# Cross attention with 128 key columns and 128 value rows where there are 77 keys

## What is computed

```python
xn1 = _ln(x, g1, be1)
sa = _mha(xn1, xn1, Wq_s, bq_s, Wk_s, bk_s, Wv_s, bv_s, causal=True)
x = x + (sa @ W1 + b1)
xn2 = _ln(x, g2, be2)
ca = _mha(xn2, encoder_out, Wq_c, bq_c, Wk_c, bk_c, Wv_c, bv_c, causal=False)
x = x + (ca @ W2 + b2)
xn3 = _ln(x, g3, be3)
ff = jax.nn.relu(xn3 @ Wf1 + bf1) @ Wf2 + bf2
return x + ff
```

## Time and profile before

| | |
|---|---|
| median of 3 runs | 603.57 us (601.41 to 603.72) |
| the profiled execution | 601.15 us, its span 599.1 us |
| mean granted clock | 0.909 |
| TensorE busy | 509.2 us, 85% of the span |
| DVE, ACT, POOL busy | 336.7, 324.5, 186.7 us |
| scores of both attentions (line 1057) | 150.0 us in 448 matmuls |
| products of both attentions (line 1086) | 108.5 us in 896 instructions |

### The profile page before, as it was taken

How to read it: one execution, slowest core, us unless ns; L and a number is a source line. 1 busy time by engine, 2 the same in 40 slices (tenths; PEclk the granted TensorE clock), 3 DMA queues, 4 the chain that set the end, 5 groups by cost and what they waited for, 6 DMA issues and landing times.

```text
span 599.1 us, 8849 instructions
## 1 busy us (share of the span) xinstructions
PE 509.2 (85%) x3296; PEld 286.1 (48%) x3296; DVE 336.7 (56%) x645; ACT 324.5 (54%) x622; POOL 186.7 (31%) x288
## 2 busy tenths in 40 slices
PE   1598875999999999999988767769999677999887
PEld 1385642343434343434333235433334356988877
DVE  3165985887878787878732035554441456263340
ACT  3685311767766767676765641346664753354460
POOL 2497950122222222222231531232324273030200
PEclk9999995999999999999998998865555978999999
DMA  8145955033352435241205045764523310101001
GB/s 280 56 137 172 219 138 91 1 64 63 65 100 55 72 63 103 59 68 34 56 4 160 18 144 105 148 146 94 110 54 75 71 42 0 36 2 36 19 19 35
DMA packets 31082, 48.11 MB, mean 80 GB/s; under 512 B 8832, under 2 KB 25728, under 8 KB 28928
## 3 DMA queue, kind: packets, MB, share of 16 engines
q1 hardware_dynamic: 30904, 47.52, 34.4%
q10 hardware_dynamic: 136, 0.03, 0.0%
HBM read 30.66 MB, written 12.03 MB: 71 GB/s over the span
## 4 chain that ended last, share of the span: by engine, by line
PE 65%; DMA 9%; DVE 9%; ACT 8%; issue 3%; POOL 2%; SPq 1%; ACTq 0%; DVEq 0%
PE ps L1086 14%; PE ps L1057 13%; PE ps L965 11%; PE ps L1020 11%; PE ps L1173 8%; DMA stacks<-shift_t 4%; DVE max_a L1252 4%; PE ps L949 3%; ACT arena_p L823 3%; DMA sums<-out_t 2%; PE ps L1042 2%; PE ps L1024 2%; ACT out_t L834 2%; ACT xn L859 1%; DMA recips<-recip_rows 1%
## 5 line engine op out<-in xcount | busy, mean ns | idle before, releaser
L823 ACT ACTIVATE arena_p<-ps 128x512 f32<-128x512 f32 (+4 forms) x416 | 197.0, 538 | 125.2 <-PE ps L1057 122.3
L1252 DVE TENSOR_REDUCE max_a<-ps 128x1 f32<-128x512 f32 (+4 forms) x280 | 163.2, 621 | 73.7 <-PE ps L1020 58.5
L1057 PE MATMUL ps<-stacks 99*128 99x512 bf16 (+2 forms) x448 | 150.0, 370 | 19.8 <-DMA stacks<-shift_t 12.5
L1020 PE MATMUL ps<-stacks 96*128 96x77 bf16 (+4 forms) x640 | 142.1, 300 | 11.0 <-DVE max_a L1252 7.8
L1086 PE MATMUL ps<-arena_p,v_group 128*32 128x512 f32 (+4 forms) x896 | 108.5, 565 | 1.6 <-POOL arena_p L694 1.2
L1020 PEld LDWEIGHTS ps<-stacks 96*128 96x128 bf16 x640 | 58.5, 112 | 95.9 <-DVE max_a L1252 44.9
L694 POOL TENSOR_SCALAR_AFFINE_SELECT arena_p<-arena_p 128x512 f32<-128x512 f32 x64 | 39.9, 635 | 176.8 <-ACT arena_p L823 176.8
L1057 PEld LDWEIGHTS ps<-stacks 99*128 99x128 bf16 (+1 forms) x448 | 46.1, 108 | 82.3 <-ACT arena_p L823 45.6
L1252 DVE TENSOR_REDUCE max_b<-ps 128x1 f32<-128x384 f32 (+3 forms) x88 | 52.4, 634 | 6.6 <-PE ps L1024 6.6
L1232 DVE TENSOR_TENSOR xs<-ps,xs 128x512 f32<-128x512 f32 x24 | 16.4, 690 | 69.1 <-PE ps L965 45.5
L899 ACT ACTIVATE hid_r<-ps,col 128x512 fp32r<-128x512 f32 x32 | 22.0, 688 | 54.2 <-PE ps L1173 51.8
(11 more groups left out here) (70 smaller groups left out, 516.9 us busy)
## 6 DMA issues: line engine op xcount, KB each, us to landing
arena_h<-out_t SPq DMA_DIRECT2D x16, 256.0 KB, 5.4
recips<-recip_rows SPq DMA_DIRECT2D x8, 512.0 KB
q_parts<-parts SPq DMA_DIRECT2D x8, 384.0 KB, 2.7
k_parts<-parts SPq DMA_DIRECT2D x8, 384.0 KB, 2.9
qc_parts<-parts SPq DMA_DIRECT2D x8, 384.0 KB, 3.2
stacks<-qc_parts SPq DMA_DIRECT2D x8, 384.0 KB, 5.4
stacks<-q_parts SPq DMA_DIRECT2D x7, 384.0 KB, 5.0
stacks<-k_parts SPq DMA_DIRECT2D x7, 384.0 KB, 7.7
```

Of the source, the lines that this page charges most:

```text
L823: nc.scalar.activation(probs[0:a.kp, a.probs_slot(g, ui), h, k * BANK:k * BANK + width], ps[0:a.kp, unit % S_BANKS, 0:width], ACT.Exp, sca ...
L1020: ins = nc.tensor.matmul(m_bank(use)[:, o:o + w], q_stack[0:ROWS, g % a.nb, h, t * P:(t + 1) * P], k_rows(ROWS, g, h, s0, s0 + w), start=T ...
L1057: ins = nc.tensor.matmul(ps[0:keys, unit % S_BANKS, lo - k * BANK:hi - k * BANK], k_rows(ROWS_S, g, h, i * P, i * P + keys), q_stack[:, g ...
L1252: nc.vector.tensor_reduce(dst, m_bank(use)[:, 0:nh * w].rearrange("p (h w) -> p h w", h=nh), AX.X, ALU.max).then_inc(s.max_read, 1)
```

## The change

Cross attention's score matmuls take 128 columns of keys for their weights, in place of 77. The keys of all groups and heads lie one behind another (`k_ctx_row`, 77 columns a head), so the columns from the 78th on are those of the next head, or, for the last, of what self attention left there. The scores then fill all 128 partitions of the bank; ACT still reads 77 of them. The products take 128 rows of V and of probs, in place of 77. For this V is filled with zeros on partitions 64 to 127 before the ones and the values are written on the first 77; and a part of `probs` that nothing has written before is cleared once, ahead of self attention. The product waits for three steps of V in place of one.

```diff
--- before.py
+++ after.py
@@ -300,8 +300,8 @@
             arena_p = attention_only.enter_context(nc.sbuf_tensor("arena_p", [P, P_SLOTS * GH * T], F32))
         q_stack = stacks[:, 0:5, :, :]
         k_self = stacks[:, 3:6, :, :]
-        k_ctx = stacks[:, 5, :, :].rearrange("p h t -> p (h t)")[:, 0:NG * GH * S_CTX]\
-            .rearrange("p (g h t) -> p g h t", g=NG, h=GH)
+        k_ctx_row = stacks[:, 5, :, :].rearrange("p h t -> p (h t)")
+        k_ctx = k_ctx_row[:, 0:NG * GH * S_CTX].rearrange("p (g h t) -> p g h t", g=NG, h=GH)
         probs = arena_p[:, :].rearrange("p (s h t) -> p s h t", s=P_SLOTS, h=GH)
 
         wf2r = sb("wf2r", [P, 2, FF // P, C], F32R)
@@ -665,6 +665,11 @@
                         src = v_self[:, g, :, :].rearrange("p i (h d) -> p i h d", d=D)
                         dst = v_group[:, g % 2, :, :, 0::2]
                     else:
+
+                        pool.wait_ge(split_p, U_QC + 6)
+                        pool.memset(v_group[64:P, 0, :, :, :], 0.0).then_inc(s.v_set, 1)
+                        pool.wait_ge(s.v_set, 1)
+                        pool.memset(v_group[0:S_CTX, 0, :, :, 1::2], 1.0).then_inc(s.v_set, 1)
                         src = v_ctx[:, :, :].rearrange("p g (h d) -> p g h d", d=D)
                         dst = v_group[0:S_CTX, 0, :, :, 0::2]
                     pool.tensor_copy(dst, src).then_inc(s.v_set, 1)
@@ -739,6 +744,10 @@
             made(pool.memset(k_self[ROWS:ROWS_S, :, :, :], 1.0))
             pool.wait_ge(consts, 9)
             third_parts(*range(12, U_QC))
+            pool.wait_ge(acc_full, 2 * a_at["v", NCH - 1] + 2)
+            pool.wait_ge(split_p, U_QC)
+            made(pool.memset(probs[64:P, 2, :, SELF.steps[2][1]:T], 0.0))
+            pool.wait_ge(consts, 10)
             attention(SELF, S1)
             add_bias(NCH)
             add_bias(NCH + 1)
@@ -1053,9 +1062,10 @@
                     for i, q0, w, off in a.steps[ui][0]:
                         lo, hi = max(off, k * BANK), min(off + w, (k + 1) * BANK)
                         if lo < hi:
-                            keys = min(P, a.keys - i * P)
-                            ins = nc.tensor.matmul(ps[0:keys, unit % S_BANKS, lo - k * BANK:hi - k * BANK],
-                                                   k_rows(ROWS_S, g, h, i * P, i * P + keys),
+                            at = (g * GH + h) * S_CTX
+                            ins = nc.tensor.matmul(ps[:, unit % S_BANKS, lo - k * BANK:hi - k * BANK],
+                                                   k_rows(ROWS_S, g, h, i * P, (i + 1) * P) if a.causal
+                                                   else k_ctx_row[0:ROWS_S, at:at + P],
                                                    q_stack[:, g % a.nb, h, q0 + lo - off:q0 + hi - off],
                                                    start=True, stop=True)
                     ins.then_inc(s.scores, 1)
@@ -1073,7 +1083,7 @@
                     else:
                         pe.wait_ge(s.exps, len(a.units) * g + GH * (n + 1))
                     if ui == 0:
-                        pe.wait_ge(s.v_set, g + 1 if a.causal else 1)
+                        pe.wait_ge(s.v_set, g + 1 if a.causal else 3)
                         at_least(pe, s.out_copied, g if a.causal else a.n_copies * (g - 1) + n + 1)
                     slot = a.probs_slot(g, ui)
                     for m, bank in parts_of:
@@ -1081,10 +1091,10 @@
                         lo, hi = max(q0, BANK * bank), BANK * (bank + 1)
                         last = i == a.kt - 1 or a.causal and bank == 0 and i == 3
                         for h in range(GH):
-                            v = v_group[0:a.kp, g % 2, i, h, :] if a.causal else v_group[0:a.kp, 0, g, h, :]
+                            v = v_group[0:a.kp, g % 2, i, h, :] if a.causal else v_group[:, 0, g, h, :]
                             o = off + lo - q0
                             ins = nc.tensor.matmul(out_region[32 * h:32 * h + 32, lo:hi], v,
-                                                   probs[0:a.kp, slot, h, o:o + hi - lo],
+                                                   probs[:, slot, h, o:o + hi - lo],
                                                    start=(i == 0), stop=last, skip_group_check=True)
                     ins.then_inc(s.pv, 1)
```

## The result

| | before | after |
|---|---|---|
| median of 11 runs each | 602.81 us (600.97 to 604.82) | 598.4 us (595.19 to 601.71) |
| profiled execution, its span | 601.15 us, 599.1 us | 595.19 us, 593.3 us |
| mean granted clock | 0.909 | 0.945 |

The ratio is 0.9929 (95%: 0.9901 to 0.9956): 4.4 us faster, where the sum had 10.1. The kernel became faster, and the time lies in the stated range of 582 to 604 us. The profiled execution is the fastest of the 11, so its trace shows more gain than the median.

A forecast was written before the change was run, and what follows sets the result against it. TensorE alone, at half clock, was taken to bound cross attention's groups. Gains of 2.2 + 6.8 + 3.2 less 2.1 gave 10.1 us, the profiled 601.15 becoming 591.0 and the median 593.5 us, range 582 to 604.

The forecast's parts named there:

- Why the clock is low there: Cross attention, 403 to 458 us: products with 77-row weights hold 1.2 GHz; with 99x128 scores and 128x32 products mostly 2.4 GHz.
- Rival D: Cross attention: the clock stays at 1.2 GHz and TensorE's time is as before, 603.6 us (603 to 605); chance 0.16.
- Step 1: Up to group 1's start at 402.91 us nothing moves, since a DMA ends the wait there.
- Step 2: Group 1 to 2: clock back near 407 us, group 2 starts at 410.3 instead of 412.5, 2.2 us gained.
- Step 6: Memsets on POOL ahead of cross attention: 1.6 us against 1.8 to spare, cost 0; the one ahead of self attention 0.
- Step 7: Behind group 7's start all is as before; norms, copies and DMAs do not hang on the width.
- Step 3: Groups 2 and 3: shift rows come late, 6.2 us each against 9.58, 6.8 us gained (8.0 or 4.0 at the ends).
- Step 4: Groups 4 to 7: reciprocals' chain on SP decides, 8.1 us from group 4 to 5; 23.6 us against 26.8, 3.2 gained.
- case A: The forecast as summed, gaps before groups ended by the shift rows' DMA: 593.5 us, own range 588 to 598; chance 0.55.
- Step 5: Last groups: TensorE idles 2 to 3 us in each, the clock falls at times; three transposes 0.7 us later, 2.1 us off.
- Rival B: Cross attention: shift rows keep up, six groups at ACT's 5.3 us, 21.7 us gained: 582 us, down to 580; chance 0.10.
- Rival C: Cross attention: clock up only in pieces after waits for shift rows, 8.3 us a group: 600 us (598 to 602); chance 0.13.

The follow-up runs named there:

- e1: The change without its edit of the scores (77 columns of weights kept, products 128 rows, memsets kept): 597.0 us, 0.9917 of the kernel before.
- e2: The change without its edit of the products and without the memsets (scores 128 columns, products 77 rows): 601.24 us, 0.9987 of the kernel before.
- e16: The change with old 77-column scores, stack loads behind the shift rows and spreads of reciprocals from ACT's queue: 594.4 us, 0.9878 of the kernel before.
- e15: The change as it is, measured a second time: 595.51 us, 0.9898 of the kernel before.
- e3: The kernel before with only the change's memsets and the wait for them, both matmuls as before: 601.59 us, 1.0001 of the kernel before.
- e9: The change with query stacks of cross attention's groups 5 to 7 loaded in only 256 of 4096 columns: 592.3 us, 0.9838 of the kernel before.
- e4: The change with V's two memsets moved right behind self attention on POOL: 599.36 us, 0.995 of the kernel before.
- e8: The change with pack, inversion, store and spread of the reciprocals issued earlier: 597.98 us, 0.9925 of the kernel before.
- e12: The change with the two spreads of reciprocals within cross attention issued from ACT's queue: 596.33 us, 0.9913 of the kernel before.
- e10: The change with both cuts, reciprocals spread for 64 of 1024 queries and small stack loads (256 of 4096 columns): 584.32 us, 0.9717 of the kernel before.
- e5: The change with cross attention's reciprocals spread for only 64 of 1024 queries (32 KB in place of 512): 592.53 us, 0.9818 of the kernel before.
- e13: The change with the three loads of a later group's stack issued behind the next group's first shift rows: 596.08 us, 0.9923 of the kernel before.

## Why the prediction was right in direction and wrong in size

**Why the clock is low there: right, with one part too much.** The products' 77 rows keep it at 1.2 GHz (e1 against e2); the scores' columns have no part in it that shows (e2, e16). Rival D (603.6) is excluded by the window at 0.91.

**Step 1: held within scatter**; group 1's start is 2.1 us later in the one trace and 1.4 later in e15 (404.29), and anywhere between 399.4 and 407.4 us elsewhere. In these two traces it is a part of what is missing all the same. **Step 2: held**, 6.8 and 6.9 us against 7.4. **Step 6: held** (e3). **Step 7: held**, the 5.4 us gained at the first W2 rows come through as 5.8.

**The step that failed is the way of the shift rows, in steps 3 and 4: its terms were sized too small.** The mechanism was that of case A, gaps ended by this DMA, and its terms measure as follows.

Step 3 took a landing of 3.4 us, hence 6.2 us for groups 2 and 3 each, and at its slow end 7.6. Measured, from issues at 413 to 416 and at 420 to 424 us of the kernel after:
```profile
stacks<-shift_t SPq DMA_DIRECT2D x3, 8.0 KB, 3.9
```
```profile
stacks<-shift_t SPq DMA_DIRECT2D x3, 8.0 KB, 5.3
```
e15 has 4.6 and 3.3. The two distances came to 15.4 (6.9 and 8.5) and 14.5 us in place of 12.4: 2 to 3 us less gained. e9 shows what was missing: with small loads of stacks the landings are 3.0 and 2.6 us, and the two distances sum to 11.3.

Step 4 took 8.1 us from group 4 to 5, and in most traces this is the largest single miss (in the kernel after, the 8.5 us of step 3's second distance is as large): 10.1 in the kernel after, 12.3 in e15, and 11.1 to 12.8 in the other kernels of this series that move only the order of DMAs or memsets (e4, e8, e12 to e16). SP's timeline in e15 shows its parts, with group 4's transpose at 426.30:
```profile
422.67 2.25 SPq L482 DMA_DIRECT2D stacks<-qc_parts  x2
424.96 0.42 SPq L511 DMA_DIRECT2D recip_rows<-sums  x1
428.38 0.66 SPq L521 DMA_DIRECT2D recips<-recip_rows  x1
429.16 0.58 SPq L428 DMA_DIRECT2D sums<-out_t  x1
429.79 0.54 SPq L436 DMA_DIRECT2D arena_h<-out_t  x1
430.37 1.85 SPq L503 DMA_DIRECT2D stacks<-shift_t  x3
```
The forecast had the first shift issue 0.9 us behind the transpose, with 0.5 for the spread. It is 4.1 us behind it. SP stands from 425.4 to 428.4 and waits for the store of 32 KB: its landing takes 3.4 us, 3.8 in the kernel after, where the earlier trace rows has 1.5. Then come the spread and the packs of sums and heads, 2.0 us, where the sum had 0.5: step 4 left out these packs for group 5, though it counted them, 1.2 us, for group 7. And then comes the landing of 6.2 us where 4.8 was taken from the earlier trace rows. Sum: 0.75 + 4.1 + 1.2 + 6.2 = 12.2 us. Why the store is slower isn't settled: it stands right behind loads of stacks here, and with small loads it still took 2.8 (e9) and 3.1 us (e10). In the kernel before the same store landed after 1.8 us, and behind spread and packs SP still had 1.1 us to spare before the first shift issue (432.83 to 433.90). That is the error: the durations were taken from a stretch in which the DMAs had 9.58 us a group, and used for one in which the same bytes go in 8.0 us a group on average (48.1 us for six); the DMA share rose from 0.43 to 0.58 in the same window. In the kernel after the clock was low at 428.59, which put that transpose 1.35 us behind the group's start, and its landing was 5.6: 1.35 + 1.8 + 1.2 + 5.6 = 10.0.

The rest of step 4 held: 5.4 and 6.9 us against 6.1, and 10.4 and 10.2 against 9.4. **Step 5** took three cold transposes, 2.1 us; the kernel after has one at 1.35 us and one at 0.97 behind a group's start, e15 has two at 1.3 (405.57 and 439.23 against 404.29 and 437.87): 1 us was taken too much, which hides part of the miss.

Over all, from group 1 to 7: 45.5 us forecast, 48.1 and 50.7 measured, 55.5 before. That is 7.5 and 4.9 us gained of 10.1 in these six distances. In the kernel after 2.1 us of it are lost again by the later start of group 1, and the span is 5.8 us shorter; in e15 1.4 are lost. The medians gained 4.4 and 5.8 us. The miss agrees with what e5 and e9 give back: the stack loads hold groups 1 to 4, the spread group 5. Rival B's 582 us was a fair account of the pace without them: e10, with nearly none of those bytes, has 584.32. Rival C took the right gaps, but in both traces of the change the clock comes back within the group in which it fell, 0.91 over the window of 413 to 450 us. Its numbers, 8.3 us a group and 598 to 602 us, are near the measured 8.0 and 8.4 us and 598.4 by luck: groups are that long by late landings and not by a cold TensorE. The same 598.4 lies just beyond the slow end of case A. Rival E fell with e3.

**Open:** why the store takes longer at the new pace; what another order gives when neither SP nor ACT waits for that store; whether the shift rows are held by the bytes of the large DMAs or by their number of packets (both cuts take away both); and whether the shift rows from GpSimd's queue would pass them, which wasn't tried. How rows and gaps together decide the clock isn't shown.

## What to carry to other kernels

When a stretch gets faster because its bound engine does, read again every transfer that was hidden in it, and don't take its old landing time for the new pace, at which the DMA engines are busier; count every transfer that stands ahead of it in the queue. The test is to shrink the transfers in both kernels and compare (2.6 us before, 11 to 13 after). A TensorE that is 100% busy may still run at half its clock: look at the granted clock beside the busy share, and try the full 128 rows, with zeros where there is no data, before changing the work. Where small DMAs that the next group needs stand behind large ones, moving them within or between two queues gave nothing here, since each order tried moved the wait to another reader; only smaller transfers did. When you move a DMA to another engine, look for every wait on the same semaphore first, as e12 shows.

## What the runs showed of the hardware that was not expected

- Products with 77 weight rows held the clock at 0.50 through 40.00 busy us of 40 (e2); with 128 rows, of which 51 are zeros in V, it was 0.78 to 0.88 over the same window with 29.5 to 33.5 us busy (e1, after, e15).
- The clock fell and rose in whole stretches. In the kernel after, the scores at 427.24 us, behind 3.02 us of idle time, ran at 0.50, and the window from 433 to 434 us has 0.78; those at 418.74 and 437.32, behind 1.40 and 1.88, at 1.00. The length of the gap alone doesn't tell: in e5, behind a gap of 1.34 us that ended at 436.66, the product at 438.25 took 1.86 us, and in the kernel after the scores right behind 3.56 us (405.00) still ran at 1.00, and the fall came 1.1 us later.
- The landing of one and the same 32 KB store ran from 1.8 us (before, e5) over 2.8 (e9) to 3.8 (after) and 5.8 (e13). Ahead of it stand two full loads in before, e5 and the kernel after, small ones in e9, three full ones in e13, so it followed the size of the loads only in part.
- 8 KB rows landed after 5.8 us behind a 512 KB spread that went out from another engine's queue (e12), as behind one from their own (5.6, 6.2).
